# Expert layer with one tile's tokens as the loaded operand, last pair tile by tile, and the FFN input transform split between engines

## The reference

```python
h = tokens(x)                                          # patches @ W.T + b
h = h + attn0(layernorm(h))                            # ternary weights, quantised activations
# expert layer, input x = layernorm(h)
probs = softmax(x @ router_w); w, idx = top_k(probs, 2); w = w / sum(w)
g, u = x @ gate_w[e], x @ up_w[e]                      # 16 experts, 512 x 192
out = sum_e combine[:, e] * ((silu(g) * u) @ down_w[e])
h = h + out
h = h + attn1(layernorm(h))                            # softmax attention, 16 heads, 4 key heads
# FFN, input x = layernorm(h)
x = fwht(x * SU_ug) / 64                               # Walsh-Hadamard transform of 512
x = silu(x @ W_gate.T * s) * (x @ W_up.T * s)          # 2048 wide
h = h + (fwht(x * SU_dp) / 64) @ W_down.T * s
```

## Time and profile before

| what | us |
|---|---|
| median of 3 runs | 288.81 |
| lowest, highest | 287.03, 289.91 |
| the profiled execution, device time | 288.17 |
| its span, first to last instruction | 286.3 |
| busy in the span: PE, DVE, ACT, POOL | 269.5, 232.0, 149.0, 9.7 |

### The profile page before, as it was taken

How to read it: one execution, slowest core, us unless ns; L and a number is a source line. 1 busy time by engine, 2 the same in 40 slices (tenths; PEclk the granted TensorE clock), 3 DMA queues, 4 the chain that set the end, 5 groups by cost and what they waited for, 6 DMA issues and landing times. The chain is left out here.

```text
span 286.3 us, 4458 instructions
## 1 busy us (share of the span) xinstructions
PE 269.5 (94%) x1704; PEld 224.8 (79%) x1707; DVE 232.0 (81%) x424; ACT 149.0 (52%) x235; POOL 9.7 (3%) x29
## 2 busy tenths in 40 slices
PE   8689569999999999999999999999999999999993
PEld 3445344859999899999989886875689999999962
DVE  1959999797997999899999856699777895777783
ACT  2997770144754665646566434344347672663530
POOL 0200000010000000000000004100100000000000
PEclk9979979999999999999999999999999999999998
DMA  6950399945080836446510068077000000000003
GB/s 248 416 228 0 93 396 400 413 203 193 30 310 23 290 149 222 161 173 215 185 40 1 2 224 362 2 282 304 0 2 0 2 1 2 0 0 2 1 0 73
DMA packets 6566, 40.45 MB, mean 141 GB/s; under 512 B 1169, under 2 KB 1425, under 8 KB 5266
## 3 DMA queue, kind: packets, MB, share of 16 engines
q1 hardware_dynamic: 6546, 40.18, 37.3%
HBM read 39.13 MB, written 0.52 MB: 138 GB/s over the span
## 5 line engine op out<-in xcount | busy, mean ns | idle before, releaser
L902 PE MATMUL bank<-s_xt_hi,s_gu_hi 128*128 128x256 f32 x120 | 34.0, 283 | 0.0
L903 PE MATMUL bank<-s_xt_lo,s_gu_hi 128*128 128x256 f32 x120 | 33.9, 283 | 0.0
L904 PE MATMUL bank<-s_xt_hi,s_gu_lo 128*128 128x256 f32 x120 | 33.9, 282 | 0.0
L1036 PE MATMUL bank<-s_xf_hi,s_f_lo 128*128 128x256 f32 x128 | 31.1, 281 | 0.0
L1036 PE MATMUL bank<-s_xf_hi,s_f_hi 128*128 128x256 f32 x128 | 31.1, 281 | 0.0
L1551 DVE TENSOR_TENSOR s_f_lo<-s_ffn_raw,s_f_hi 128x1024 fp32r<-128x1024 f32 x16 | 19.6, 1225 | 6.6 <-ACT s_f_hi L605 6.5
L1036 PEld LDWEIGHTS bank<-s_xf_hi,s_f_hi 128*128 128x128 f32 x128 | 24.1, 188 | 0.4
L1036 PEld LDWEIGHTS bank<-s_xf_hi,s_f_lo 128*128 128x128 f32 x128 | 24.1, 188 | 0.3
L902 PEld LDWEIGHTS bank<-s_xt_hi,s_gu_hi 128*128 128x128 f32 x120 | 23.0, 191 | 0.2
L903 PEld LDWEIGHTS bank<-s_xt_lo,s_gu_hi 128*128 128x128 f32 x120 | 22.9, 191 | 0.2
L904 PEld LDWEIGHTS bank<-s_xt_hi,s_gu_lo 128*128 128x128 f32 x120 | 22.9, 191 | 0.0
(11 more groups left out here) (249 smaller groups left out, 679.4 us busy)
## 6 DMA issues: line engine op xcount, KB each, us to landing
s_moe_raw<-moe_gu SPq DMA_DIRECT2D x16, 768.0 KB, 5.9
s_ffn_raw<-ffn_w SPq DMA_DIRECT2D x4, 2048.0 KB, 9.9
s_moe_raw<-moe_dn SPq DMA_DIRECT2D x8, 768.0 KB, 4.5
s_big_raw<-att_w SPq DMA_DIRECT2D x4, 1024.0 KB, 8.2
s_big_raw<-down_w SPq DMA_DIRECT2D x1, 4096.0 KB, 20.0
s_l_raw<-l_w SPq DMA_DIRECT2D x1, 2560.0 KB, 25.6
out<-s_h SPq DMA_DIRECT2D x4, 128.0 KB, 2.3
s_tok_w<-tok_w SPq DMA_DIRECT2D x1, 256.0 KB, 2.9
```

Of the source, the lines that this page charges most:

```text
L902: pe.matmul(dst, w_hi, xt_hi[:, k, :], start=(k == 0), stop=False)
L903: pe.matmul(dst, w_hi, xt_lo[:, k, :], start=False, stop=False)
L904: last = pe.matmul(dst, w_lo, xt_hi[:, k, :], start=False, stop=(k == KC - 1))
L1036: pe.matmul(tb(j, n)[:, 0:TOK], M[w][j][:, k, n * P:(n + 1) * P], M["xf_hi"][:, k, :], start=(w == "w_hi" and k == 0), stop=False)
```

## The change

**Experts.** A unit is now one expert and one tile: 32 units, four a pair. The tile's tokens (128) are the loaded operand and the expert's 384 gate and up columns move: 12 matmuls of 384 columns. Hidden values come out with tokens on partitions, so the combine weight is one number a partition: VectorE does SiLU times weight times up in one instruction of 192 columns. `combine`, `sel`, `ct` and their matmuls are gone. Hidden values have to be transposed now: 3 transposes a tile and pair (`hidden_transposes`), split from PSUM in two steps of 384 columns.

**Router.** Its 16 columns are appended to expert 0's weights, so both units of expert 0 move 400 columns and bring the scores with them. The first four units are multiplied before the combine weights exist and scaled afterwards (`scaled`).

**Last pair.** Tile 0's two units, its transposes and its `dn` are done before tile 1's second unit, the down weights are split chunk by chunk (`last_dn_high`, `last_dn_low`), and tile 0's layernorm lies beside tile 1's work. Queries of tile 1 come before its keys and values; turns are re-ordered (4 and 5 at the experts' end, 6 and 7 after the projections, 9 and 10 before `values(1)`, 11 and 12 inside it).

**FFN input.** `across_chunks` on VectorE multiplies by the signs (a row made by 4 matmuls ahead of the experts) and does the additions between the four 128-wide chunks; the division by the standard deviation is a diagonal matrix (`scaled_identity`) in the transposing matmuls, now plain fp32; TensorE does 8 matmuls of 256 columns instead of 32. The last fold's first step stands ahead of `xt_low(9)`, the rest after the FFN's input is split.

The core of the diff:

```diff
+            def unit(i):
+
+                e, t = UNIT[i]
+                pe.wait_ge(gu_ready, e + 1)
+                if i >= 4:
+                    pe.wait_ge(mul_done, i - 3)
+                for k in range(KC):
+                    x, w = xt(k, t), [B[name][e % 2][:, k, 0:GU] for name in ("w_hi", "w_lo")]
+                    last = split_products(unit_bank(i)[:, 0:GU], x, w[0], w[1], k == 0, k == KC - 1)
+                last.then_inc(gu_done, 1)
...
+            for p in range(2, PAIRS - 1):
+                unit(4 * p)
+                hidden_transposes(p - 1, 0)
+                unit(4 * p + 1)
+                hidden_transposes(p - 1, 1)
+                unit(4 * p + 2)
+                dn(p - 1, 0)
+                unit(4 * p + 3)
+                dn(p - 1, 1)
...
+            unit(4 * PAIRS - 1)
+            dn(PAIRS - 1, 1, 0, 1)
+            hidden_transposes(PAIRS - 1, 1, 1, 3)
+            transposes(4, L["xn"], 0)
             turn(4)
+            dn(PAIRS - 1, 1, 1, 3)
             turn(5)
...
+            def across_chunks(t, src):
+
+                xn, y = M["xn"], M["y"]
+                half = C // 2
+                o.settle(t)
+                o.mark(dve.scalar_tensor_tensor(xn[:, t, :], src, mv[:, t, 0:1], su_row[:], ALU.subtract, ALU.mult), t)
+                o.settle(t)
+                o.mark(dve.tensor_tensor(y[:, 0:half], xn[:, t, 0:half], xn[:, t, half:C], ALU.add), t)
+                o.mark(dve.tensor_tensor(y[:, half:C], xn[:, t, 0:half], xn[:, t, half:C], ALU.subtract), t)
...
+            def lane_transform(j, x, first):
+
                 for i in (2 * j, 2 * j + 1):
...
+                    last = pe.matmul(tb(j, 2)[:, i % 2 * TOK:(i % 2 + 1) * TOK], had[:], x[:, i, :],
+                                     start=(first and i % 2 == 0), stop=(not first and i % 2 == 1))
```

More of the change, by code:

```diff
@@ L838, in _, with unit_products @@
             turn(3)
-            keep_warm(bank[3], 2)
+            pe.wait_ge(ld_small, 48)
+            for k in range(KC):
+                last = pe.matmul(bank[6][:, k * P:(k + 1) * P], su_c[:, k:k + 1].to_broadcast([P, P]), ident,
+                                 start=(k == 0), stop=(k == KC - 1))
+            last.then_inc(su_done, 1)
+            def unit_products(i, part, first, last):
+                e, t = UNIT[i]
+                n = GU + (0 if e else E)
+                w = B[("w_hi", "w_hi", "w_lo")[part]][e % 2]
+                for k in range(KC):
+                    ins = pe.matmul(unit_bank(i)[:, 0:n], xt(k, t)[part % 2], w[:, k, 0:n],
+                                    start=(first and k == 0), stop=(last and k == KC - 1))
+                if last:
+                    ins.then_inc(gu_done, 1)
@@ new lines, in _ @@
+            unit(6)
+            hidden_transposes(0, 1)
+            dn(0, 0)
+            unit(7)
+            dn(0, 1)
+            for p in range(2, PAIRS - 1):
+                unit(4 * p)
[6 more added lines that the diff above has]
+                dn(p - 1, 1)
+            unit(4 * PAIRS - 4)
+            hidden_transposes(PAIRS - 2, 0)
@@ L978, in values @@
                 for s in range(keys):
+                    if t == 1 and s > 0:
+                        turn(10 + s)
                     pe.wait_ge(val_ready, 2 * t + s + 1)
@@ L1362, in _ @@
             main_low(1)
-            top, tops = B["top"], B["tops"]
+            rest_low(1)
             def over_e(ap):
@@ L1516, in _ @@
+            hidden(6)
+            main_low(4)
+            rest_low(4)
+            hidden(7)
+            for p in range(2, PAIRS - 1):
+                main_low(2 * p + 1)
+                rest_low(2 * p + 1)
+                hidden(4 * p)
+                dn_low(p - 1)
+                hidden_low(p - 1, 0)
+                hidden(4 * p + 1)
+                hidden_low(p - 1, 1)
                 fold_piece(p - 1)
+                hidden(4 * p + 2)
+                main_low(2 * p + 2)
+                rest_low(2 * p + 2)
@@ L1545, in _ @@
+            moments(0)
+            hidden_low(PAIRS - 1, 1, 0, 1)
+            normalised(2, 0, L["xn"]).then_inc(xn_ready, 1)
+            hidden(4 * PAIRS - 1)
+            hidden_low(PAIRS - 1, 1, 1, 3)
+            xt_low(4)
+            experts_added(1)
+            moments(1)
             normalised(2, 1, L["xn"]).then_inc(xn_ready, 1)
-            xt_low(4)
             xt_low(5)
```

692 lines of the change are left out of this document (331 added, 361 removed).

## The result

| | us |
|---|---|
| changed kernel, median of 4 runs | 291.79 (291.30 to 293.51) |
| kernel before, 4 runs beside it | 288.73 (287.03 to 289.91) |
| ratio, 95% interval | 1.0121 (1.0077 to 1.0165) |
| profiled execution of the changed kernel, its span | 291.70, 289.9 |

The account below looks back on a forecast made before the run. TensorE bounds the experts, chains between engines layer 1's attention. Last dn's end 172.9 plus 39.4 gives FFN start 212.3; with the FFN unchanged 288.1, plus 1.0 for the clock 289.2, set at 289.5 between two bases; range 285.3 to 291.8 us.

Parts of the forecast that it names:

- The price of a matmul and the pair: TensorE in the experts: 0.1735 us per 384-column matmul, middle pair 13.01 us against 13.06, 0.25 us less over five pairs.
- Experts' start: Up to pair 2's first unit: it starts at 88.2 us instead of 90.42, a gain of 2.2.
- The three waits: TensorE waiting for VectorE in the first expert units: unit 4 0.4 us, unit 6 0.5, first dn 1.0.
- Experts' end: From unit 28 to the last dn's end (T): 19.6 us; T at 172.9 against 173.16, a gain of 0.3.
- The second softmax: Layer 1's attention: ScalarE's copies delay the exponential to T (last dn's end) + 22.0; TensorE idles 2.6 us before values(1).
- The clock: Behind the pause before values(1): clock falls to 1.2 GHz, slowing the next three microseconds' work, costing 0 to 1.7 us.
- I take 1.0: The charge for the clock's fall behind the pause before values(1): 1.0 us, between bounds of 0 and 1.7.
- FFN input: From tile 1's output product's end to the FFN's start: 7.4 us, with TensorE idling 0.2, 1.0, 0.4 and 0.7.
- FFN: FFN's start to the span's end: unchanged, 74.0 us; start expected at 211.5 to 214 us.
- Even: Whole kernel: the pause before values(1) does not slow the clock; 288.1 us, or 288.5 by the median; chance 0.28.
- Slower: The clock falls a second time, on the FFN's dense start, after idling at its input: +1.7, 291.2 us; chance 0.14.
- Faster by smaller pauses: Softmax pause and waits at the experts' beginning taken away: 283.9 us, one of the two about 286; chance 0.19.

Follow-up runs that it names:

- experiment 8: Changed kernel without two of three hidden transposes per tile in pairs 1 to 5 (hidden values wrong): 289.25 us, 1.0006 of the kernel before.
- experiment 2: Changed kernel with the second softmax's exponential ahead of the copies of turns 9 and 10 on ScalarE: 287.45 us, 0.9952 of the kernel before.
- experiment 4: Kernel before with the second softmax's exponential put behind the copy of turn 10 on ScalarE: 290.40 us, 1.0059 of the kernel before.
- experiment 1: Changed kernel measured again, unaltered: 291.54 us, 1.0083 of the kernel before.
- experiment 9: Changed kernel, softmax exponential first, turn 6 ahead of tile 1's swap: 287.07, again 286.13 us; also with FFN-input fillers 286.86, with old FFN input 288.07.
- experiment 7: Changed kernel with filler matmuls (6 and 4) in the FFN input's two pauses only: 291.67 us, 1.0102 of the kernel before.
- experiment 5: Changed kernel with the old FFN input (signed blocks by GpSimd, plain transposes, 32 matmuls): 291.39 us, 1.0077 of the kernel before.
- experiment 6: Changed kernel with hidden(31) ahead of the normalising of layer 1's tile 0 on VectorE: 290.17 us, 1.0063 of the kernel before.

## Why the prediction was wrong

The step that failed is the size of two terms, TensorE's own work and the slow clock, and not the chain that the prediction described. The forecast's terms add to a span of 287.3 us; the measured one is 289.9. Of the 2.6 us between them 1.4 are the matmul and transpose prices (1.0 in the middle pairs, 0.4 at the experts' end), 0.65 is the clock, and some 0.5 is spread over T to values(1) (0.16), the FFN input (0.15) and the FFN (0.2). One by one:

- **The price of a matmul and the pair.** 384 columns: 0.1735 (0.170 to 0.180) forecast, 0.176 measured. A transpose: 0.58 for six forecast, 0.65 measured. The pair: 13.01 forecast, 13.22 measured (inside 12.9 to 13.3), which makes a loss of 0.16 a pair out of a gain of 0.05. 512 columns: 0.228 forecast, 0.231 measured. Five pairs: 1.0 us of the missing 2.6. The mechanism was right (TensorE alone, no releaser named in the middle pairs, experiment 8), the term was mis-sized: each piece was taken at or near its cheapest row. The Trainium skill ("TensorE: Matmul & The Clock Gate", section Back-to-back issue gap) gives columns / 2.4 + 2.5 ns for the gap of single matmuls, an estimate of 162.5 ns for 384 columns. The trace has 176, and the measurement decides.
- **Experts' start.** Pair 2 at 88.22, forecast 88.2. The three waits were there and smaller than forecast: unit 4 for `s_hm` 0.17 us (0.4 forecast), unit 6's weight load for `s_w_lo` 0.16 (0.5), the first dn for `s_ht_lo` 0.59 (1.0). The units began later (69.31 for 69.05) and were longer, which cancelled. That 88.2 came out to the tenth is luck.
- **Experts' end.** 20.0 us from unit 28 to T, forecast 19.6; the hidden transposes late by about what was said (0.75 from the last dn matmul to them). The prices measured in the middle, over four units, two dns and twelve transposes, account for the 0.4. T is 174.33 for 172.9.
- **The second softmax.** Forecast: exponential at T + 22.0, values(1) at T + 23.7 with 2.6 us idle. Measured: T + 21.9 and T + 23.9, 2.5 us. Right, and shown by experiments 2 and 4. The pause was in the sum in full; the gains set against it were too large, since 0.25 us gained in the middle pairs became 0.8 lost and T came 1.2 us later than before, not 0.3 earlier.
- **The clock.** That it would fall there was right; "I take 1.0" was the mis-sized step. Without the fall the stretch behind takes 8.27 to 8.31 us, with it 9.94: 1.65 us, the prediction's outer bound of 1.7. The slow stretch began as values(1) did and lay wholly on work of the chain; nothing of it fell into the pause. In experiment 1 it began later (the first eight matmuls and their turn take 2.19 us there, not 3.21) and cost the same, 9.95 us in all. 0.65 us of the missing 2.6.
- **FFN input.** 7.55 us, forecast 7.4, with idle times at two of the places named (0.67 and 0.54 us). It is a gain of the change (experiment 9: 0.8 us), not a loss.
- **FFN.** 74.2 us, forecast 74.0. It starts at 215.68, behind the 211.5 to 214 that the prediction gave as a sign. The chunks with a down product behind them stand 4.24 to 4.25 us apart, before 4.22 to 4.23; the cause stays open.
- **The rivals.** "Even" fell with the clock, which went to 0.57 behind the pause. "Slower" had the right time (291.2) and the wrong mechanism: the changed kernel's profile has the clock at 1.00 at the FFN's start (212 to 216), and fillers there change nothing (experiment 7). "Faster by smaller pauses" fell with the softmax pause.

So of the 3.6 us between the spans, the change gains 2.2 at the experts' start and 0.9 at the FFN input (8.41 against 7.55), and loses 0.8 in the middle pairs, 2.4 by one line's place on ScalarE and 1.65 by the clock that this brings with it. The rest is a loss of some 1.7 us: 2.6 more between pair 2 and T beside the middle pairs (1.3 of it moved there), 2.0 less from T to values(0), 0.2 less from there to values(1), 1.1 more behind values(1), where turns 11 and 12 now lie inside it, and 0.2 in the FFN. It was not taken apart further, and no experiment tests these pieces.

## What to carry to other kernels

When work is moved on one engine, look at what the other engines have queued ahead of an instruction whose input does not need that work: an exponential of 0.26 us behind two copies cost 4.1 us with what followed from it, as much as 37 transposes of 0.11 us. A pause of TensorE costs twice where the clock falls behind it: here 2.4 us of pause and 1.6 us of slow matmuls, so count the whole slow stretch if what follows is on the chain, and give the fall a chance and not a certainty, since the same pause does not always bring it. In a stretch that TensorE fills, price every form by the distance over a whole run of them and across the seams between forms, not by the best row.

## What the runs showed of the hardware

The same pause (values(0) to values(1) 10.8 us) made the clock fall at values(1) in the profiles of the changed kernel twice and of experiments 5, 6 and 7, and not in that of experiment 8, where values(1) came 1.6 to 3.4 us earlier than in those. In the five the stretch behind took 9.94 to 9.95 us wherever in it the slow part began, in the sixth 8.29. There the clock fell behind the FFN's start instead:

```profile
211.00:215.00 4.00, 4.00 (x22) 4.00 (x22) 2.84 (x4) 0.66 (x3) 0.00 (x0) 0.57 0.00 0
```

The clock also goes with most of the spread of one and the same program. The fall at 14 to 17 us is not in every execution; this is the version of experiment 9 with fillers, whose program is the changed kernel's far beyond this place:

```profile
14.00:17.00 3.00, 2.77 (x18) 1.25 (x17) 2.43 (x9) 3.00 (x3) 0.00 (x0) 1.00 1.04 392
```

The changed kernel's profile has 0.54 there. In the four microseconds ahead TensorE was busy for nearly the same time, 2.28 us where the clock stayed and 2.33 where it fell. The clock at 38 to 41 us differs too (0.71 and 0.50). Pair 2 starts at 86.78 us in the first and at 88.22 in the second. Among 35 runs of the kernel before, the nine with a mean clock of 0.994 took 287.05 to 288.77 us and the eight with 0.975 or 0.976 289.82 to 291.09. The Trainium skill ("TensorE: Matmul & The Clock Gate", section Part 1: The HAM clock gate) says that the moment of the transition varies between runs; these runs agree. For a comparison by half a per cent, stretches of the trace behind a common start were worth more here than medians of a few runs.
